# A graph network's edge stage on one core: source rows transposed into a PSUM bank of their own and added on VectorE, and one bank for two layers

## The reference, cut to what matters

```
h     = silu(edge_attr @ fc1 + b1)            # 32 -> 128
h     = silu(h @ fc2 + b2)
scale = h @ fc3 + b3
msg   = silu(x[src] @ W_node * scale + edge_sh @ W_sh)
a     = silu(concat(x[src,:64], x[dst,:64], edge_attr) @ aW1 + ab1)
a     = silu(a @ aW2 + ab2)
a     = a @ aW3 + ab3                          # 8 scores an edge
```

## Time and profile before

| what | value |
|---|---|
| three executions | 4978.45, 5012.18, 5027.13 us |
| the profiled execution: own time | 5044.25 us |
| its span (first to last instruction) | 5042.4 us |
| busy in the span: TensorE, VectorE, ScalarE, GpSimd | 75%, 37%, 31%, 36% |
| edge stage (110 to 1215 us of the span) | 1105 us for 100 chunks |

### The profile page before, as it was taken

The page is one execution under the profiler, slowest core; times in us unless marked ns, Lnnn a source line. Parts: engine busy times, 40 slices in busy tenths (PEclk is TensorE's granted clock), DMA queues, the critical chain, the costliest instruction groups (busy, mean ns, idle before and its releaser), DMA issues. The chain is left out here.

```text
span 5042.4 us, 83052 instructions
## 1 busy us (share of the span) xinstructions
PE 3763.8 (75%) x23281; PEld 2288.7 (45%) x23281; DVE 1851.4 (37%) x5399; ACT 1538.0 (31%) x3573; POOL 1837.9 (36%) x1815
## 2 busy tenths in 40 slices
PE   3788777875754787777477787766677777999998
PEld 1455555543542444444344444433444444555564
DVE  4444444444753333333223333332232222335223
ACT  2333333332232333333233333322222222313112
POOL 1333333331033555555245555435545553000000
PEclk7888788887976898988788989877888787999999
DMA  3344444444755333333344455434434443554223
GB/s 108 106 121 125 114 123 121 123 117 77 238 171 169 79 93 90 85 90 89 81 113 122 118 132 129 111 89 107 107 101 108 107 106 80 172 180 157 83 89 121
DMA packets 673822, 586.67 MB, mean 116 GB/s; under 512 B 379103, under 2 KB 527621, under 8 KB 672901
## 3 DMA queue, kind: packets, MB, share of 16 engines
q1 hardware_dynamic: 579886, 377.56, 26.6%
q0 software_dynamic: 77008, 200.24, 15.0%
q10 hardware_dynamic: 16768, 6.91, 0.5%
HBM read 471.65 MB, written 112.79 MB: 116 GB/s over the span
## 5 line engine op out<-in xcount | busy, mean ns | idle before, releaser
L1967 POOL DMA_INDIRECT aw_y<-s_lrows,aw_src x1350 | 1379.7, 1022 | 1284.6 <-PE ps L2034 689.4
L2034 PE MATMUL ps<-aw_y,aw_pT 128*63 128x277 f32 x2700 | 481.8, 501 | 331.8 <-ACT aw_pT L2218 202.9
L742 POOL DMA_INDIRECT em_gs<-s_rows,em_idx x400 | 385.0, 963 | 699.3 <-DMA em_idx<-in_sd 539.0
L2943 PE MATMUL ps<-nl_adj,nl_table 126*128 126x504 bf16 (+1 forms) x3150 | 631.8, 357 | 2.3 <-DVE nl_table L3178 2.3
L1994 PE MATMUL ps<-ident,aw_y 128*128 128x128 f32 x2700 | 454.6, 308 | 188.3 <-DVE aw_y L2330 82.3
L2204 ACT ACTIVATE aw_yT<-ps 128x512 f32<-128x512 f32 x675 | 386.0, 597 | 365.3 <-remote 174.1
L1994 PEld LDWEIGHTS ps<-ident,aw_y 128*128 128x128 f32 x2700 | 344.4, 158 | 336.2 <-issue 177.9
L2018 PE MATMUL ps<-aw_yT,aw_qt 128*63 128x384 f32 x1800 | 372.0, 520 | 158.3 <-ACT aw_yT L2204 111.6
L2365 DVE COPY aw_axd<-ps 128x252 f32<-128x252 f32 x225 | 94.7, 421 | 1071.4 <-PE ps L2051 583.1
L2034 PEld LDWEIGHTS ps<-aw_y,aw_pT 128*63 128x63 f32 x2700 | 211.1, 165 | 524.2 <-issue 248.0
L2943 PEld LDWEIGHTS ps<-nl_adj,nl_table 126*128 126x128 bf16 x3150 | 301.9, 96 | 299.3 <-issue 6.1
(11 more groups left out here) (374 smaller groups left out, 6089.5 us busy)
## 6 DMA issues: line engine op xcount, KB each, us to landing
nl_adj<-s_adj SPq DMA_DIRECT2D x20, 3100.8 KB
aw_geoS<-s_geoS SPq DMA_DIRECT2D x450, 94.5 KB
nl_adj<-s_adj SPq DMA_DIRECT2D x15, 2325.6 KB
ws_msg<-s_msg SPq DMA_DIRECT2D x75, 384.0 KB, 3.9
aw_qt<-s_qt SPq DMA_DIRECT2D x225, 126.0 KB
s_msg<-em_msg SPq DMA_DIRECT2D x100, 256.0 KB
aw_y<-s_lrows,aw_src POOLq DMA_INDIRECT x1350
s_adj<-em_adj SPq DMA_DIRECT2D x75, 258.4 KB
```

Of the source, the lines that this page charges most:

```text
L742: pool.indirect_dma_start(out=gs[:, u, j, :], out_offset=None, in_=d["rows0"], in_offset=bass.IndirectOffsetOnAxis(ap=idx[:, u, 2 * j:2 * ...
L1967: pool.indirect_dma_start(out=y[:, u, j, 0:W], out_offset=None, in_=table, in_offset=bass.IndirectOffsetOnAxis(ap=src[:, u, j:j + 1], axis ...
L2034: m = nc.tensor.matmul(k.ps[64 * v:64 * v + HW, SUM, 0:SW], pT[:, SLOT[u], j, 64 * v:64 * v + HW], y[:, u, v * TH + j, 0:SW], start=j == 0 ...
L2943: m = nc.tensor.matmul(k.ps[:, bank(i, p), 0:cols * WN], source[:, p, q, b, :], adj[:, a % 2, 0:cols, b * WN:(b + 1) * WN], start=b == 0 a ...
```

## The change

In `begin` the four source-row products no longer add in AB. They are transposes into a bank GB (the old HB2), they come before the destinations' product, and they signal a step G of their own. ScalarE copies GB to SBUF (g0). VectorE's new `join` adds AB and g0 into a0. ScalarE's silu of A1 reads a0. VectorE runs `join(c)` after `one_hot` and `keys` and before `finish(c-1)`. FC2 goes to HB, the bank of FC1. The wait for gathered rows stands before the waits for the table and the one-hot.

```diff
-        early = Steps(sem("early"), ["FC1", "A1", "FC2", "A2"], U)
+        early = Steps(sem("early"), ["FC1", "G", "A1", "FC2", "A2"], U)
-        act_ = Steps(sem("act"), ["H1", "A1", "H2", "A2"], U)
+        act_ = Steps(sem("act"), ["H1", "G", "A1", "H2", "A2"], U)
+        joined = Steps(sem("joined"), ["A0"], U)
-        HB, AB, SCALE, SHB, A3, ADJ, HB2 = 0, 1, 2, 3, 4, 5, 7
+        HB, AB, SCALE, SHB, A3, ADJ, GB = 0, 1, 2, 3, 4, 5, 7
...
+                if fast:
+                    pe.wait_ge(rows_in[u], (i + 1) * 64)
+                else:
+                    pe.wait_ge(gathered.sem, gathered.of(c, "GA"))
+                for j in range(4):
+                    m = nc.tensor.transpose(k.ps[:, GB, j * 128:(j + 1) * 128], gs[:, u, j, D:2 * D] if fast else ga[:, u % 2, j, :],
+                                            k.ident[:, :])
+                m.then_inc(early.sem, 1)
                 if fast:
                     pe.wait_ge(tab_in[u], (i + 1) * 16)
                     pe.wait_ge(picked.sem, picked.of(c, "PICK"))
                     nc.tensor.matmul(k.ps[:, AB, :], tab[:, u, :], pick[:, u % 2, :].rearrange("p (q j) -> p j q", j=4),
-                                     start=False, stop=False)
-                    pe.wait_ge(rows_in[u], (i + 1) * 64)
+                                     start=False, stop=True).then_inc(early.sem, 1)
-                for j in range(4):
-                    m = nc.tensor.matmul(k.ps[:, AB, j * 128:(j + 1) * 128], gs[:, u, j, D:2 * D] if fast else ga[:, u % 2, j, :],
-                                         k.ident[:, :], start=False, stop=j == 3)
-                m.then_inc(early.sem, 1)
...
-                nc.tensor.matmul(k.ps[:, HB2, :], fc2[:, :], h1[:, b, :], start=True, stop=True).then_inc(early.sem, 1)
+                nc.tensor.matmul(k.ps[:, HB, :], fc2[:, :], h1[:, b, :], start=True, stop=True).then_inc(early.sem, 1)
...
             def layers1(c, u):
                 layer(c, u, "FC1", HB, h1, 0)
-                layer(c, u, "A1", AB, a1, 2)
+                act.wait_ge(early.sem, early.of(c, "G"))
+                act.sem_inc(hop["act"], 1)
+                act.wait_ge(joined.sem, joined.of(c - 1, "A0"))
+                nc.scalar.activation(g0[:, :], k.ps[:, GB, :], ACT.Copy).then_inc(act_.sem, 1)
+                act.wait_ge(joined.sem, joined.of(c, "A0"))
+                nc.scalar.activation(a1[:, u % 2, :], a0[:, :], ACT.Silu, bias=bias[:, 2:3]).then_inc(act_.sem, 1)
...
+            def join(c):
+                dve.wait_ge(early.sem, early.of(c, "A1"))
+                dve.sem_inc(hop["dve"], 1)
+                dve.wait_ge(act_.sem, act_.of(c, "G"))
+                nc.vector.tensor_tensor(a0[:, :], k.ps[:, AB, :], g0[:, :], ALU.add).then_inc(joined.sem, 1)
...
+                    join(c)
                     finish(c - 1, (u - 1) % U)
```

More of the change, by code:

```diff
@@ L586, in edge_messages @@
         h1, h2, a1, a2 = (sb(n, [128, 2, CE]) for n in ("h1", "h2", "a1", "a2"))
+        g0, a0 = (sb(n, [128, CE]) for n in ("g0", "a0"))
         t1, t2, t3, msg = (sb(n, [128, 2, 4, D]) for n in ("t1", "t2", "t3", "msg"))
@@ L764, in begin @@
                 nc.tensor.matmul(k.ps[:, HB, :], fc1[:, :], feat[0:EA, u, :], start=True, stop=True).then_inc(early.sem, 1)
-                nc.tensor.matmul(k.ps[:, AB, :], aw1e[EA:EW_, :], feat[EA:EW_, u, :], start=True, stop=False)
+                nc.tensor.matmul(k.ps[:, AB, :], aw1e[EA:EW_, :], feat[EA:EW_, u, :], start=True, stop=not fast)
                 if not first:
                     sh_product(c - 1, (u - 1) % U)
+                if fast:
[6 more added lines that the diff above has]
+                m.then_inc(early.sem, 1)
                 if fast:
@@ L771, in begin @@
                     nc.tensor.matmul(k.ps[:, AB, :], tab[:, u, :], pick[:, u % 2, :].rearrange("p (q j) -> p j q", j=4),
-                                     start=False, stop=False)
-                    pe.wait_ge(rows_in[u], (i + 1) * 64)
-                else:
-                    pe.wait_ge(gathered.sem, gathered.of(c, "GA"))
-                for j in range(4):
-                    m = nc.tensor.matmul(k.ps[:, AB, j * 128:(j + 1) * 128], gs[:, u, j, D:2 * D] if fast else ga[:, u % 2, j, :],
-                                         k.ident[:, :], start=False, stop=j == 3)
-                m.then_inc(early.sem, 1)
+                                     start=False, stop=True).then_inc(early.sem, 1)
+                else:
+                    pe.sem_inc(early.sem, 1)
             def finish(c, u):
@@ L852, in layers1 @@
                 layer(c, u, "FC1", HB, h1, 0)
-                layer(c, u, "A1", AB, a1, 2)
+                act.wait_ge(early.sem, early.of(c, "G"))
[4 more added lines that the diff above has]
+                nc.scalar.activation(a1[:, u % 2, :], a0[:, :], ACT.Silu, bias=bias[:, 2:3]).then_inc(act_.sem, 1)
             def layers2(c, u):
-                layer(c, u, "FC2", HB2, h2, 1)
+                layer(c, u, "FC2", HB, h2, 1)
                 layer(c, u, "A2", AB, a2, 3)
@@ L900, in sums_of_ends @@
                 dve.wait_ge(rows_in[u], (i + 1) * 128)
-                dve.wait_ge(early.sem, early.of(c - 2, "A1"))
+                dve.wait_ge(early.sem, early.of(c - 2, "G"))
                 nc.vector.tensor_tensor(ga[:, u % 2, :, :], gs[:, u, :, D:2 * D], gd[:, u, :, :], ALU.add).then_inc(gathered.sem, 1)
+            def join(c):
[3 more added lines that the diff above has]
+                nc.vector.tensor_tensor(a0[:, :], k.ps[:, AB, :], g0[:, :], ALU.add).then_inc(joined.sem, 1)
             def nodes(i):
@@ L985, in body @@
                     select(1, 1, 0)
+                    join(0)
                     keys(0)
@@ L995, in _ @@
             gathered.prime(dve)
+            joined.prime(dve)
             picked.prime(dve)
```

## The result

The kernel before took 5003.5 us (median of ten executions, 4978 to 5027), the changed one 5044.9 us (ten, 4993 to 5062): ratio 1.0072, 95% interval 1.0041 to 1.0103. By that ratio the change costs 36 us, by the two medians 41. 5047 us had been forecast.

What follows compares the result with a forecast made beforehand. It took the edge stage's rounds to be pinned by gathers and stalls, with TensorE's saving worth 0. One term, 1.54 us in 23 rounds or +35 us, on the median 5012.18 gave 5047 us, range 4955 to 5105.

Steps and rivals of the forecast that it cites:

- the sum: Edge stage, turn 3: one term, 1.54 us in 23 rounds, +35 us, bounds 0 and 60.
- The place: Turn 3: join behind select and three pairs of one-hots, delaying silu of A1 and L805; message 1.54 us later.
- The trigger: Turn 3: the engines' stall during the gathers holds the join until 598.88, making the message 1.54 us later.
- rival 2: Turn 3: join gets in ahead of the stall or during it, chain as long as before; 5012 us, chance 0.15.
- a sign of being wrong: Turn 3: the forecast is wrong if the join starts before the stall; no size given.
- Pinned rounds, saving worth 0: Edge stage: stalls pinned to the gathers, so almost all of TensorE's 60 us saving is waited away; 0, bounds 0 and 60.
- Rival 1: Edge stage: TensorE sets the pace, saving counts in turns 0, 1 and 2; 45 us gained, 4967 us, chance 0.17.
- Turn 1 at most 0.2 us: Turn 1: L805 starts as before despite copy, join and silu; 0 us, at most 0.2.
- turn 2 hidden: Turn 2: the added chain of 1.4 us is hidden behind 2.2 us of TensorE work.
- Rival 3, the clock: Edge stage: low clock lasts longer after the stalls, turn 1 low too; 91 us more, 5103 us, chance 0.15.
- The shared bank: FC2 into HB, the bank of FC1, waits for nothing new; costs nothing, without cover 0.69 us a turn.
- the moved waits: Wait for gathered rows moves ahead of two others, but rows are gathered four chunks ahead; costs nothing.

Runs made afterwards that it cites:

- select_last: Changed kernel with VectorE's select, which waits for the load of the edges' ends, moved behind finish: ratio 0.9838 to the kernel before.
- more_pe: Kernel before with FC2 in FC1's bank and four extra transposes a chunk, read by nobody: ratio 1.0023 to the kernel before.
- join_first: Changed kernel with the join moved to the head of VectorE's turn, ahead of the next chunk's one-hots: ratio 1.0082 to the kernel before.

## Why the prediction was right or wrong

- *The number.* +35 us on the median was forecast, +36 measured (1.0072). That it fits so well is luck: the sum was 1.54 us in 23 rounds, from a join caught by the stall, and the one trace of that chip shows no join caught and no longer stage.
- *The place.* "Turn 3 ... the join stands behind select ... and three pairs of one-hots", with L805 late behind it and at the low clock at 1.91 us: right in both runs of the changed kernel without stalls, with the late product at 2.07 us. There the turn's loss was 3.8 us, not 1.54.
- *The trigger.* This step failed. The text had the join caught by the stall ("the next instruction did not start until 598.88"). In the profile after, it got in ahead, as rival 2 said and as the text had named as a sign of being wrong. The row that carries the cost was in the prediction, and read as a detail: select "waited for an edge load". Without any stall, that wait of 3.7 us ahead of the join is what turn 3 loses by: with select moved behind it, turn 3 takes 6.91 us.
- *Pinned rounds, saving worth 0.* With the stalls this held: TensorE had less to do and the round stayed at 44.1 us. (In the trace of the kernel before, two turns 3 ran without the stall, 7.6 and 7.9 us, not one.) Without the stalls TensorE is the pace in turns 1 and 2, and the saving shows there, 0.3 us a turn or some 15 us in all. Rival 1 thus had its mechanism but not its sign.
- *Turn 1 at most 0.2 us, turn 2 hidden*: held; turn 2 went from 6.52 to 6.2 us.
- *Rival 3, the clock.* It had more to it than its chance of 0.15 says. On the chip of the forecast the stage was granted 0.78 instead of 0.82. Without the stalls it was 0.86 instead of 1.00 from 300 to 500 us, with turn 0 at the low level in more than half of the rounds. What went before was TensorE standing still for A1 in turn 3, 3.01 us before the L810 that took 2.07, and 70.6 us in 25 waits from 110 to 820 us. The transposes weren't the cause: with them in every turn but no such wait, select_last was granted 0.99 between 300 and 500 us, and the kernel before with the same move 1.00. By these two figures, four transposes a turn among the products go with a granted clock lower by 0.01; a stretch of transposes alone was not run.
- *The shared bank, the moved waits*: the bank cost nothing, as forecast, by the bound that more_pe gives. The wait for the gathered rows cost 4.2 us in all in the profile after, but 33.8 us in select_last, where the rows no longer came in time.

Open: where the 36 us lie on the chip of the first comparison. The only profile of the changed kernel there is its fastest execution, and in it the edge stage isn't longer. An ordinary one was not seen, since no later run met the stalls; nor was their cause. One hint: the granted clock over the whole of an execution was 0.852 in the profiled one and down to 0.841 in the others of its ten, and 0.853 in the profiled one of the kernel before. More of the low clock, as in the runs without stalls, would cost time; that it is the 36 us isn't shown.

## What to carry to other kernels

Before a new step joins a critical chain, look at what stands ahead of it in its engine's program and what that waits for: a load's wait that nobody minded becomes the chain's, as select's 3.71 us did here. Putting the step first isn't the cure if the step itself must wait (188.4 us for the copy in join_first, turn 3 at 8.64 us); move the waiting instruction behind (6.91 us, from 12.05). Count the low clock that comes after a wait too: here it reached into the next turn, where the first product took 1.21 us and not 0.69. Where TensorE was made lighter, the gain showed in the turns in which it had been the pace: 0.3 us each in turns 1 and 2.

## What the runs showed that had not been expected

The same kernel took 5003 us in the first comparison and 3886 to 3893 us on three other chips, with 44.2 and 29.8 us a round. The difference sits in the two stages with indirect gathers (1116 and 776 us, 2697 and 1883), and not in the last stage (759 in both). Whether it is the chip or something else about that first occasion no run tells. Ratios between kernels moved with it, 1.007 and 1.014 for the same pair.
